# Four graph layers on one core: the start, the order of the loads, and how the tiles of the second layer are split and transposed

## The reference

```python
def _L0_gnn_ref(H, adj, W, b):
    H_ = jnp.einsum('nd,hde->hne', H, W)
    out = jnp.einsum('nm,hme->hne', adj, H_) + b[:, None, :]
    return jnp.transpose(out, (1, 0, 2)).reshape(H.shape[0], HEADS * DPH)
...
x = _layernorm(x + _L0_gnn_ref(x, adj, L0_gnn_W, L0_gnn_b), axis=-1)
x = _layernorm(x + _L1_gnn_ref(x, adj, L1_gnn_W, L1_gnn_a), axis=-1)
x = _layernorm(x + _L2_gnn_ref(x, adj, L2_gnn_W1, L2_gnn_b1, L2_gnn_W2, L2_gnn_b2), axis=-1)
x = _layernorm(x + _L3_gnn_ref(x, adj, L3_gnn_W), axis=-1)
```

## Time and profile before

| | |
|---|---|
| median of 3 runs | 685.93 us (685.82 to 686.82) |
| the profiled execution's own time | 686.31 us |
| its span, first to last instruction | 684.6 us |
| mean granted TensorE clock over the span | 0.997 |
| TensorE busy | 673.4 us, 98% of the span |
| VectorE, ScalarE, GpSimd busy | 521.6, 388.8, 166.2 us |
| moved by the DMA engines | 47.65 MB |

### The profile page before, as it was taken

One profiled execution on the slowest core, in us unless ns is written; L12 is line 12 of the kernel. 1 busy time (PEld: TensorE's weight loads), 2 busy tenths in 40 slices (PEclk: granted clock), 3 DMA queues, 4 the chain that ended last, 5 costly groups with the idle time before them and its releaser, 6 DMA issues.

```text
span 684.6 us, 14405 instructions
## 1 busy us (share of the span) xinstructions
PE 673.4 (98%) x5326; PEld 512.5 (75%) x5326; DVE 521.6 (76%) x965; ACT 388.8 (57%) x499; POOL 166.2 (24%) x260
## 2 busy tenths in 40 slices
PE   8989999999999999999999999999999999999996
PEld 6878744888888888888888888884444468886444
DVE  4257668998998989989899898999454425874685
ACT  6556448898979889898898979643101000222000
POOL 4369717601000000000100001664021102442222
PEclk9999999999999999999999999999999999999998
DMA  8999431003003030030300303013021111211011
GB/s 307 402 407 300 85 105 37 16 1 82 13 33 61 27 65 0 31 61 31 61 0 31 61 0 63 1 37 72 17 54 24 24 23 17 40 39 32 32 51 42
DMA packets 48153, 47.65 MB, mean 70 GB/s; under 512 B 36016, under 2 KB 42224, under 8 KB 45936
## 3 DMA queue, kind: packets, MB, share of 16 engines
q1 hardware_dynamic: 45664, 39.37, 19.0%
q0 software_dynamic: 2016, 7.34, 5.7%
q10 hardware_dynamic: 432, 0.39, 0.2%
HBM read 29.23 MB, written 2.13 MB: 46 GB/s over the span
## 4 chain that ended last, share of the span: by engine, by line
PE 93%; DMA 4%; ACT 1%; DVE 1%; POOL 0%; issue 0%; SPq 0%; ACTq 0%; POOLq 0%
PE ps L720 17%; PE ps L722 16%; PE ps L721 16%; PE ps L566 16%; PE ps L556 9%; PE ps L669 6%; PE ps L568 6%; PE ps L569 6%; DMA arena<-in_adj 4%; ACT adj L408 1%; DMA arena<-in_x_turned 1%; PE ps L546 0%; DVE x L784 0%; POOL rstd L1182 0%; DVE total L894 0%
## 5 line engine op out<-in xcount | busy, mean ns | idle before, releaser
L722 PE MATMUL ps<-arena,ring_hl 128*128 (+1 forms) x1024 | 279.7, 273 | 0.0
L720 PE MATMUL ps<-arena,ring_hl 128*128 (+1 forms) x1024 | 278.9, 272 | 0.0
L721 PE MATMUL ps<-arena,ring_hl 128*128 (+1 forms) x1024 | 278.6, 272 | 0.0
L1043 DVE SCALAR_TENSOR_TENSOR ring_a<-rho,gam,ring_a 128x1024 f32<-128x1024 f32 x128 | 164.9, 1288 | 18.0 <-ACT ring_a L463 18.0
L1048 DVE TENSOR_TENSOR ring_hl<-ring_a,ring_hl 128x1024 f16<-128x1024 f32 x128 | 157.2, 1229 | 4.9 <-ACT ring_hl L477 4.8
L477 ACT ACTIVATE ring_hl<-ring_a 128x1024 f16<-128x1024 f32 x128 | 135.2, 1056 | 43.6 <-PE ps L722 29.2
L463 ACT ACTIVATE ring_a<-adj,shift 128x1024 f32<-128x1024 bf16 x128 | 145.6, 1138 | 0.0
L568 PE MATMUL ps<-arena,adj 128*128 128x257 f16 (+1 forms) x512 | 113.1, 273 | 2.6 <-ACT adj L408 2.6
L569 PE MATMUL ps<-arena,adj 128*128 128x256 f16 x512 | 113.1, 273 | 0.0
L566 PE MATMUL ps<-arena,adj 128*128 128x512 f16 x496 | 111.6, 379 | 0.0
L721 PEld LDWEIGHTS ps<-arena,ring_hl 128*128 128x128 f16 x1024 | 99.1, 97 | 13.8
(11 more groups left out here) (109 smaller groups left out, 589.3 us busy)
## 6 DMA issues: line engine op xcount, KB each, us to landing
arena<-in_adj SPq DMA_DIRECT2D x16, 1024.0 KB, 10.9
x<-y POOLq DMA_DIRECT2D x14, 512.0 KB, 5.2
rho<-s_scratch SPq DMA_DIRECT2D x8, 512.0 KB, 3.7
x<-in_x SPq DMA_DIRECT2D x4, 512.0 KB, 16.3
out_x<-x SPq DMA_DIRECT2D x16, 128.0 KB, 1.7
arena<-in_x_turned SPq DMA_DIRECT2D x2, 512.0 KB, 7.5
arena<-in_L_gnn_W SPq DMA_DIRECT2D x1, 1024.0 KB, 10.6
arena<-in_L_gnn_a SPq DMA_DIRECT2D x1, 1024.0 KB, 12.5
```

The source lines that it names most:

```text
L720: nc.tensor.matmul(acc, hi, v_hi, start=(jt == 0), stop=False)
L721: nc.tensor.matmul(ps[:, b, 0:D], hi, v_lo, start=False, stop=False)
L722: ins = nc.tensor.matmul(acc, lo, v_hi, start=False, stop=(jt == T - 1))
L1043: nc.vector.scalar_tensor_tensor(a, rho[:, q, :], gam[:, at(h, 1), jt], a, op0=ALU.max, op1=ALU.mult)\
```

## The change

It does the following.

- **Start.** `XT_LOADS` is cut otherwise: tiles (0), (1), (2,3), (4 to 7), (8 to 11), (12 to 15) in place of (0), (1 to 3), (4,5), (6,7), (8 to 11), (12 to 15). Tile 1 is issued by ScalarE. The piece (8 to 11) is issued when (2,3) has landed, the first block of `adj` when (4 to 7) has. WARM is 36. VectorE takes over two of ScalarE's high halves (tiles 12, 13 and 14, 15), and casts blocks 0 and 2 behind tiles 11 and 15 in place of 8 and 11.
- **L0.** `project(0, t)` for all 16 tiles, then the first four output tiles in the order of `FIRST_LOADS`: tiles 0 and 1 with block 0, tiles 2 and 3 with block 2, then 0 and 1 with block 1, 2 and 3 with block 3.
- **Loads.** Blocks 6 and 7 come before `w1f` and `abc`, `x(2)` behind block 9, `x(3)` behind block 11.
- **Orders.** ScalarE casts up to block 7 before its first `gat_hi`, makes `w1_hi` behind `gat_hi(3)` and casts block n behind `gat_hi(n-5)`. VectorE's `weight_lo` and `was_lo` move to the turns of tiles 12 and 13, and the first four tiles are interleaved. GpSimd makes `product(t-3)` and `add_b0(t+2)`, and from tile 9 on the low half of tile t-1.
- **Slots and transpositions.** `xg` has 16 slots (the second eight lie over `rho`), and `gat_hi` waits for no transposition. Transposition t waits for t-4 (TURNS = 4), in all layers.

```diff
-    WARM = 28
+    WARM = 36
+    TURNS = 4
...
-        xg = part(y[:, :, :].rearrange("p a f -> p (a f)"), (0, BANKS * D), F16, "p (s q f) -> p s q f", s=BANKS, q=2)
+        xg = [part(v, (0, BANKS * D), F16, "p (s q f) -> p s q f", s=BANKS, q=2)
+              for v in (y[:, :, :].rearrange("p a f -> p (a f)"), r_flat)]
...
-        XT_LOADS = [(0, 1), (1, 4), (4, 6), (6, 8), (8, 12), (12, 16)]
+        XT_LOADS = [(0, 1), (1, 2), (2, 4), (4, 8), (8, 12), (12, 16)]
...
-            return s_tc[t % 2], 16 * ((k - 1) * T // 2 + t // 2 + 1)
+            return s_tc[t % TURNS], 16 * (((k - 1) * T + t) // TURNS + 1)
...
-                sp.dma_start(xts[:, lo:hi, :], xt_in[:, lo:hi, :]).then_inc(ld_xt[n], 16)
+                if n == 4:
+                    sp.wait_ge(*xt_loaded(2))
+                if n != 1:
+                    sp.dma_start(xts[:, lo:hi, :], xt_in[:, lo:hi, :]).then_inc(ld_xt[n], 16)
...
+            sp.wait_ge(*xt_loaded(4))
             for n in FIRST_LOADS:
                 load_adj(n)
...
+            load_adj(6)
+            load_adj(7)
             sp.wait_ge(s_lo, T)
...
-            load_adj(6)
-            load_adj(7)
+            load_adj(8)
+            load_adj(9)
             load_x(2)
-            load_adj(8)
-            load_x(3)
-            for n in range(9, NL - 2):
+            for n in range(10, NL):
                 load_adj(n)
-            for n in range(NL - 2, NL):
-                load_adj(n)
-
+                if n == 11:
+                    load_x(3)
             for t in range(T):
-                if t >= 2:
-                    sp.wait_ge(*turned(1, t - 2))
+                if t >= TURNS:
+                    sp.wait_ge(*turned(1, t - TURNS))
...
+            act.dma_start(xts[:, 1:2, :], xt_in[:, 1:2, :]).then_inc(ld_xt[1], 16)
...
-                if t >= BANKS:
-                    act.wait_ge(*turned(1, t - BANKS))
-                nc.scalar.activation(xg[:, t % BANKS, 0, :], x[:, t, :], ACT.Copy).then_inc(s_hi, 1)
-            for n in (1, 3, 4, 5):
+                nc.scalar.activation(xg[t // BANKS][:, t % BANKS, 0, :], x[:, t, :], ACT.Copy).then_inc(s_hi, 1)
+            for n in (1, 3, 4, 5, 6, 7):
                 cast_n(n)
-            w1_hi(0)
-            w1_hi(1)
-            cast_n(6)
             CAST = cast_n
-            behind = {0: [(CAST, 7)], 2: [(CAST, 8)], 3: [(CAST, 9)], 4: [(CAST, 10)], 5: [(CAST, 11)], 6: [(CAST, 12)],
-                      7: [(CAST, 13)], 9: [(CAST, 14)], 10: [(CAST, 15)], 12: [(was_hi,)]}
+            behind = {3: [(w1_hi, 0), (w1_hi, 1)], 11: [(was_hi,)]}
+            for n in range(8, NL):
+                behind.setdefault(n - 5, []).append((CAST, n))
...
-            joint(0, 0, lambda t: 0, columns_cast)
+            for t in range(T):
+                project(0, t, t % R)
+            pe.wait_ge(s_one, 1)
+            for n in FIRST_LOADS:
+                pe.wait_ge(*cast_done(n))
+                for j in range(n % 2 * JH, (n % 2 + 1) * JH):
+                    if n < 2:
+                        pe.wait_ge(s_c, j + 1)
+                    for it in (n // 2 * 2, n // 2 * 2 + 1):
+                        agg_step(0, 0, it, it, j, j == T - 1)
...
-            fill[8].append(lambda: weight_lo(1, w1, w1ff, [0]))
-            fill[9].append(lambda: weight_lo(1, w1, w1ff, [1]))
-            fill[13] = [was_lo]
+            fill[12] = [lambda: weight_lo(1, w1, w1ff, [0]), was_lo]
+            fill[13] = [lambda: weight_lo(1, w1, w1ff, [1])]
...
-            for t in range(T + 2):
+            for t in range(T + 1):
                 if t < T:
                     inv_std(t, t % R)
-                if t >= 2:
-                    prep_lo(1, t - 2, (t - 2) % R, x)
-                if 0 <= t - 2 < 4 * K2:
-                    product(t - 2)
-                if R <= t < T - R:
-                    add_b0(t + R)
+                for n in (t - 2,) if t < 9 else (7, 8) if t == 9 else (t - 1,):
+                    if n >= 0:
+                        prep_lo(1, n, n % R, x)
+                if 0 <= t - 3 < 4 * K2:
+                    product(t - 3)
+                if 2 * R <= t + 2 < T:
+                    add_b0(t + 2)
```

More of the change, by code:

```diff
@@ L164, in graph_stack @@
         s_warm = sem("s_warm")
-        s_tc = [sem(f"s_tc{i}") for i in range(2)]
+        s_tc = [sem(f"s_tc{i}") for i in range(TURNS)]
         s_accp, s_sump, s_vp = sem("s_accp"), sem("s_sump"), sem("s_vp")
@@ L274, in _ @@
                          a_in.rearrange("h f a -> a (h f)").partition_broadcast(P)).then_inc(ld_a, 16)
[L275 to L276 removed]
+            load_adj(8)
+            load_adj(9)
             load_x(2)
[L278 to L280 removed]
+            for n in range(10, NL):
                 load_adj(n)
[L282 to L283 removed]
+                if n == 11:
+                    load_x(3)
             for t in range(T):
[L286 to L287 removed]
+                if t >= TURNS:
+                    sp.wait_ge(*turned(1, t - TURNS))
                 sp.wait_ge(s_lo, T + t + 1)
                 sp.dma_start_transpose(xt[:, t, :].rearrange("p (c i) -> p c i", c=2 * K2),
[L290 removed]
+                                       xg[t // BANKS][:, t % BANKS, :, :].rearrange("p q f -> p (q f)"))\
+                  .then_inc(s_tc[t % TURNS], 16)
             sp.wait_ge(s_cap, 1)
@@ L319, in _ @@
                 for t in range(T):
-                    if t >= 2:
-                        sp.wait_ge(*turned(k, t - 2))
+                    if t >= TURNS:
+                        sp.wait_ge(*turned(k, t - TURNS))
                     if k == 2 and t % R == 0:
@@ L328, in _ @@
                     sp.dma_start_transpose(xt[:, t, :].rearrange("p (c i) -> p c i", c=2 * K2),
-                                           xs[:, t % R, :, :].rearrange("p q f -> p (q f)")).then_inc(s_tc[t % 2], 16)
+                                           xs[:, t % R, :, :].rearrange("p q f -> p (q f)"))\
+                      .then_inc(s_tc[t % TURNS], 16)
             def store(t, u):
@@ L394, in _ @@
             w0_hi(1)
-            for chunk in CHUNKS[1:6]:
-                turned_hi(*chunk)
-            turned_after = {0: 6, 1: 7, 3: 8, 5: 9}
+            turned_hi(*CHUNKS[1])
+            turned_hi(*CHUNKS[2])
+            turned_after = {0: CHUNKS[3:5], 1: CHUNKS[5:6], 2: CHUNKS[6:7], 3: CHUNKS[7:8]}
             for t in range(T):
                 take_p(0, t, t % R)
-                if t in turned_after:
-                    turned_hi(*CHUNKS[turned_after[t]])
+                for chunk in turned_after.get(t, []):
+                    turned_hi(*chunk)
             for n, bi in enumerate((b1_in, b2_in)):
@@ L953, in turned_lo, with turned_hi @@
                 nc.vector.tensor_sub(xt[:, lo:hi, D:2 * D], xts[:, lo:hi, :], xt[:, lo:hi, 0:D]).then_inc(s_lo, hi - lo)
+            def turned_hi(lo, hi):
+                dve.wait_ge(s_hi, lo)
+                dve.wait_ge(*xt_loaded(lo))
+                nc.vector.tensor_copy(xt[:, lo:hi, 0:D], xts[:, lo:hi, :]).then_inc(s_hi, hi - lo)
             turned_lo(*CHUNKS[0])
@@ L958, in _ @@
                                                op0=ALU.mult, op1=ALU.subtract).then_inc(lo_made, 1)
-            for chunk in CHUNKS[1:5]:
-                turned_lo(*chunk)
-            casts_after = {8: 0, 11: 2}
+            turned_lo(*CHUNKS[1])
+            turned_lo(*CHUNKS[2])
+            casts_after = {11: 0, 15: 2}
+            turned_after = {3: 8, 5: 9}
             for t in range(T):
                 take(0, t, t % R)
+                if t == 0:
+                    turned_lo(*CHUNKS[3])
+                    turned_lo(*CHUNKS[4])
                 if t in casts_after:
                     cast_n(casts_after[t])
+                if t in turned_after:
+                    turned_hi(*CHUNKS[turned_after[t]])
             def weight_lo(n, buf, src, halves=range(K2)):
@@ L982, in _ @@
             fill = {t: [lambda t=t: sum_products(t - R)] for t in range(R, R + 4 * K2)}
-            fill[8].append(lambda: weight_lo(1, w1, w1ff, [0]))
-            fill[9].append(lambda: weight_lo(1, w1, w1ff, [1]))
-            fill[13] = [was_lo]
+            fill[12] = [lambda: weight_lo(1, w1, w1ff, [0]), was_lo]
+            fill[13] = [lambda: weight_lo(1, w1, w1ff, [1])]
             lines = [stages(0, 1, t, t) for t in range(R)]
-            for line in lines:
-                line[0][0]()
-            for early, late_ in lines:
-                for st in early[1:] + late_:
+            for t, phase in ((0, 0), (1, 0), (0, 1), (2, 0), (1, 1), (3, 0), (2, 1), (3, 1)):
+                for st in lines[t][phase]:
                     st()
```

9 lines of the change are left out of this document (1 added, 8 removed).

## The result

The changed kernel takes **688.27 us** (median of 10 runs, 687.05 to 689.29) against 685.88 us for the kernel before in the same series (10 runs, 685.47 to 686.84): a ratio of 1.0031, 95% interval 1.0022 to 1.0040. It is slower, by 2.4 us, where I had forecast 2.7 us faster and a range that ended at 685.0. Its profiled execution took 688.47 us with a span of 686.4 us (before 686.31 and 684.6); 2.07 us lie around the span, 1.71 before.

What follows compares the result with a forecast made beforehand. TensorE was busy 673.4 of 684.6 us, so its start of L1, held by late loads, was taken to decide; 2.9 - 0.1 - 0.1 = 2.7 us off the median 685.93 gave 683.2 us, range 681.5 to 685.0.

Steps and rivals of the forecast that it cites:

- Rival B: At the start: the new waits let the transfer queue run dry; later blocks and `abc` slip 0.8 to 2 us; chance 0.14.
- A: Rival: the transfer queue is quicker at the start, landings up to 2 us earlier, time 681.0 to 682.4 us; chance 0.13.
- Loads, -2.9 us: Before L1: quarters of `x` go behind block 9, which lands at 47.49, not 50.42; L1 could begin at 76.1.
- The waits, taken at 0: On SP's queue at the start: no change assumed up to block 3, with 1 MB or more still queued at either wait.
- The sums, +0.1: Before L1: chain from `abc` landing at 42.5 has the weights' second half ready at 76.2; takes 0.1 us of the gain.
- Rival C: Before `project(1, 0)`: sums become the bound, L1 at 82.9, time 689.8 us; decides from a turn of 3.9 us; chance 0.06.
- The transposed tile 14, +0.1: In L1: tile 14 is needed 7.8 us in and transposed at 7.9; 0.1 us more taken off the gain.
- The beginning: Aggregation of L0 starts at 17.4 against 19.43; the 2 us won are cover if the clock rises late, not gain.
- Four in flight, cost and gain zero: Transpositions behind the last block: two in flight already give one per 1.3 us, four give the same.

## Why the prediction was wrong

**What failed is the sentence on which the cost of the two waits hung**: "I think 1 MB or more is still queued at either wait." With it went "I take no change there" for the queue up to block 3. Rival B named the mechanism, had 0.14, and was priced at 0.8 to 2 us of slip and 684.0 to 685.2 us. It was right in kind and too cheap. The sentence held when the waits began (1.2 and 1.1 MB), but not when they ended: 0.26 and 0.9 MB were left, and 0.3 where the second wait stood alone. And 0.9 MB was not enough to keep the rate up. Blocks and `a` slipped by 1 us up to block 3, 3 us at block 4, 3.7 at `a` (2.2 in another execution), and the time by 2.8. The rule of the Trainium skill that I quoted there (DMA: Bandwidth & Descriptors, Rules for kernel authors: issue early, wait late) was the better guide, and the runs with and without the waits agree with it. The price was bounded by one lone piece's latency, 2.5 us at most; that 0.5 to 0.9 MB more would go past `a` stood in no row of before.

One slip stands in the range: the middle of A is 681.7 and the end of B 685.2, not 681.5 and 685.0.

From 683.2 to 688.3 are 5.1 us. Step by step:

- **Loads, -2.9 us.** Sized right as a landing of block 9 (47.33 in the kernel before with its loads reordered, 47.38 in the change without SP's waits), wrong as a gain. Alone it is worth nothing: the floor of block 6, and the last casts behind the sums, took it back. It needs `w1f` and `a` behind block 7 as well, which my sum had, and the later high halves, which it had not.
- **The waits, taken at 0.** 2.8 us.
- **The sums, +0.1.** The step was turns of 3.54, "then half a weight of 1.27 in a turn of 2.91". Measured:

```profile
48.02 0.75 DVE L792 TENSOR_SCALAR x<-total,mv,rstd 128x256 f32<-128x256 f32 x1 [0.55 <-POOL rstd L1198]
...
49.94 0.69 DVE L956 TENSOR_REDUCE wa<-ring_a 128x2 f32<-128x512 f32 x1 [0.83 <-POOL ring_a L1191]
...
51.66 0.75 DVE L792 TENSOR_SCALAR x<-total,mv,rstd 128x256 f32<-128x256 f32 x1 [0.56 <-POOL rstd L1198]
...
78.55 1.41 DVE L990 SCALAR_TENSOR_TENSOR w<-arena,w 128x1024 f16<-128x1024 f32 x1
```

  A turn is 3.64 us (51.66 - 48.02), and inside it VectorE waits 0.83 for the product. The first half weight took 1.41 and the turn with it 3.45. From the first product at 44.55 to the end of the second half, 79.96, are 35.4 us where I had 33.7; 1.0 of the 1.7 lies behind tile 11, in the two turns with the halves. Without SP's waits L1 began at 76.39, next to the forecast of 76.2, and that is luck: `a` landed at 40.7, 1.8 us earlier than the 42.5 that I took, and the chain behind it was as much too long. Rival C, sums as the bound with a slower end, named the place (`project(1, 0)` waiting for the weights) but not the size: it needed turns of 3.9. Undoing this was worth 0.7 us without the waits and 1.7 with them.
- **The transposed tile 14, +0.1.** It cost 0.6 us in the change and in nearly every variant.
- **The beginning.** "They are cover" was right: TensorE ran through from 1.06 to 10.1 us, and the old beginning is as fast. The start of the aggregation was 1.6 us later than said, and not because the piece (8 to 11) was held back: without the waits it is 18.93. GpSimd's low halves ended at 16.67 where my sum has 15.5 (9.7 + 5 x 1.15): in the change it stood 1.4 us for the piece (8 to 11), and without the waits (4 to 7) landed at 9.0 and GpSimd began at 10.66. And TensorE, paused before, still had eight of the sixteen tiles to project at 13.7 in both runs, 5.2 us, which my sum had not. Around the span 0.3 us were added, which no row of before could price.
- **Four in flight, cost and gain zero**: no run shows otherwise.

With the waits gone and the products late the profiled span is 681.7 us, and my forecast of the span was 681.9; but that execution is one of the two shortest of its twelve, whose median span is 682.7. The 5.1 us are then 2.8 for the waits, 0.7 for the sums, and 1.6 that stay in this last version: 0.8 because its typical span is above the forecast, 0.35 around the span, and 0.4 because I had taken the profiled execution to be 0.4 above the median.

## What to carry to other kernels

Do not hold a transfer back behind a landing to give an earlier one the queue: of the 1 MB that was queued when a wait began, 0.26 to 0.9 MB was left when it ended, the rate fell, and a hole of 0.5 MB by 12 us became 2.2 to 3.7 us at 44 us. An edit that only moves transfers should be priced at the next two limits too: here the late block had a floor two blocks earlier and a cast behind another engine's sums, and alone it gave nothing. When a load is moved so that a chain hangs on it, count the whole chain from that landing, with durations from the places where both engines run together.

## What the runs showed that I had not expected

The queue that was held back for some microseconds did not only lose what it had not moved. 0.9 MB more of later transfers than without the waits were through before `a`, over 30 us after the last wait (0.5 MB in another execution).

A stop of 2.45 us brought TensorE's clock to its lower level for the 3.4 us that eight matmuls then took, 1.7 more than at full clock. Two shorter stops had no such cost: behind the one of 1.62 us that ends at 48.99 in the change, and behind the one of 1.86 us that ends at 41.87 in the run with the loads' order alone, the granted clock of the next 3.5 us is 1.00.

The clock at the beginning differs from run to run of the same code. Behind 28 warm-up matmuls the first tile's six matmuls took 1.46 us before and 0.84 in the run with the loads' order alone, and that aggregation began at 18.64 and not 19.43, with the same beginning.
